# Token stages with centring and variance as 64x64 blocks in four tiles of the array, and token products padded to 128 rows

## The chip, the cores and the metric

The kernel runs on one core of one Trainium2 chip. The metric is the device time of one execution in microseconds (us). TensorE (PE in the profile) does the matrix products, its weight loads stand apart as PEld; ScalarE is ACT, VectorE is DVE, GpSimd is POOL, and SyncE (SP) issues nearly all DMAs.

## What is computed

The reference is a block of two layers over an image of 4 x 48 x 128 x 128. Each layer is a convolution part and a token part; the change touches the token part, which is the same for both layers:

```python
x = x + _L0_conv_ref(_ln_c(x), ...)
t = _to_tokens(x)                                  # B, H*W, C = 48 channels per token
t = t + _L0_ffn_ref(_ln_t(t), W1, b1, W2, b2)
x = _from_tokens(t, x)
x = x + _L1_conv_ref(_ln_c(x), ...)
...
def _ln_t(v, eps=1e-05):                           # over the 48 channels
    m = jnp.mean(v, axis=-1, keepdims=True)
    s = jnp.var(v, axis=-1, keepdims=True)
    return (v - m) / jnp.sqrt(s + eps)

def _qlinear(x, W, b):                             # 8-bit floats in, 16-bit floats out
    y = q_acc(jnp.einsum('bsk,nk->bsn', q_mul(x), q_mul(W)))
    return q_acc(y + q_mul(b))
h = jax.nn.relu(_qlinear(x, W1, b1))               # 48 -> 192
y = _qlinear(h, W2, b2)                            # 192 -> 48
```

## The kernel before

The program is a row of stages, each with its own buffers and a barrier of all engines behind it: `expand`, `gated_conv`, `token_mix` ("mix0"), `wavelet`, `attention_maps`, `fusion`, and `token_mix` again ("mix1"). Only `token_mix` changes. I call its two calls the first and the second token stage. The first is `wide` (its source has 96 rows) and has a second layer norm over its result, `"out"`, whose output feeds the wavelet stage; the second has the norm `"in"` only.

A token stage works through 2N = 64 tiles of 512 tokens. A tile holds two images at once: channels of one on partitions 0 to 47, of the other on 64 to 111 (`PADH` = 64, `CP` = 112). For one tile these pieces run, each on one engine:

- `project` (PE): the projection of the conv part into `x1_bank`; `add_residual` (DVE) adds the input and gives `x1`.
- `centre_in` (PE, L871): a 112x112 product with `center` subtracts the mean over each image's 48 channels; `square` (ACT, L934); `variance("in")` (PE, L889): a 112x112 product with `average`, into `x1_bank` again; `root` (ACT, L941 and L944): Ln and Exp give the reciprocal root; `quantize_norm` (DVE, L1030) multiplies and rounds to 8 bits, `xq`.
- `hide(0)`, `hide(1)` (PE, L902): 48 to 192 for both images, four products of 96 output rows, each into a bank of its own out of `bank` (two banks in the first stage, four in the second); `round_hidden` (ACT, L951) copies each bank to 16 bits; `bias_hidden` (DVE, L1036) and `quantize_hidden` (DVE, L1046) give `hq`.
- `show` (PE, L914): four accumulating products back to 48 channels in `x2_bank`; `round_shown` (ACT, L957); `add_shown` (DVE, L1052, L1057) adds `x1` and gives `x2`, which SP stores.
- in the first stage also `centre_out` (PE, L877), `square("out")`, `variance("out")` (PE, L889, into `x2_bank`), `root("out")` and `normalise` (DVE, L1066).

`staged` sets the order. Every engine walks over steps; in step k it takes its pieces in the order of the list `pieces`, each with the tile k minus that piece's stage number. So one step holds one piece of each kind, of different tiles, and each engine's order within a step is fixed by hand:

```python
pieces = [(0, project), (3, show), (2, hide(0)), (4, centre_out), (2, hide(1)), (1, variance("in")), (5, variance("out")), (0, centre_in)]
```

The engines wait for one another only by counting semaphores, written ahead of each piece (`pe.wait_ge(...)`). Which wait holds which piece decides the length of a step. Ahead of the loop DVE fills paddings with zeros, the last fill (L981) raises `prepared`, and SP, which waits for it, then issues the weights' DMAs and behind them the first tile's.

## Time and profile before

| | |
|---|---|
| median of 3 runs | 2580.16 us (2574.28 to 2590.53) |
| the profiled execution, its own time | 2568.33 us |
| its span, first to last instruction | 2566.5 us |
| mean granted TensorE clock, share of full speed | 0.94 |
| PE, DVE, ACT, POOL busy | 88%, 59%, 46%, 17% of the span |
| first token stage | about 793 to 1275 us |
| second token stage | about 2203 to 2566 us |

The profiled execution lies 2.18 us above its span. A busy share is a mean over stages with different limits, so it is read stage by stage: the timeline of one step of either token stage tells which engine waits there, and for what.

### The profile page before, as it was taken

How to read it: one execution, taken by the hardware profiler on the slowest of the kernel's cores; microseconds unless marked ns; L12 is line 12 of the kernel's file. 1: busy time of each engine (PE TensorE's matmuls, PEld its weight loads, DVE VectorE, ACT ScalarE, POOL GpSimd, SP SyncE). 2: the span in 40 equal slices, each digit the busy share in tenths (PEclk: the TensorE clock that was granted, in tenths of full speed). 3: DMA queues.
4: the chain of work that ended last, by engine and by line, in shares of the span. 5: the costliest groups of instructions: out<-in, count | busy, mean ns of one | idle time of the engine just before them, and what ended most of it. 6: DMA issues, size and time to landing. Idle time of an engine off the chain costs nothing. (4 is left out here: it accounts for less than half of the span.)

```text
span 2566.5 us, 61875 instructions
## 1 busy us (share of the span) xinstructions
PE 2261.6 (88%) x21290; PEld 1261.1 (49%) x21290; DVE 1521.9 (59%) x2653; ACT 1175.5 (46%) x2386; POOL 448.9 (17%) x707
## 2 busy tenths in 40 slices
PE   7679859999996999999699999999984999699997
PEld 3335517785783333333266666666651342233333
DVE  3335501111113777777578888888871555488887
ACT  4346422222222888888622222222220221388887
POOL 7610006101100000000044444444420000000000
PEclk9789859999997999999899999999996999799999
DMA  6999987787754778777486666666635999344343
GB/s 151 263 253 271 244 283 236 272 268 240 262 190 93 142 144 153 141 146 149 88 159 144 145 145 145 145 145 145 143 88 125 244 263 268 111 114 116 111 114 89
DMA packets 529401, 445.99 MB, mean 174 GB/s; under 512 B 315708, under 2 KB 444676, under 8 KB 525938
## 3 DMA queue, kind: packets, MB, share of 16 engines
q1 hardware_dynamic: 459042, 413.28, 62.6%
q0 software_dynamic: 5744, 23.34, 3.6%
q10 hardware_dynamic: 64512, 7.88, 2.3%
q8 instruction: 79, 1.29, 0.2%
q14 instruction: 24, 0.20, 0.0%
HBM read 259.75 MB, written 186.40 MB: 174 GB/s over the span
## 5 line engine op out<-in xcount | busy, mean ns | idle before, releaser
L602 PE MATMUL gate_ps<-gate_data,gate_wt 64*64 64x289 f32 x6144 | 389.2, 410 | 25.7 <-issue 18.9
L602 PEld LDWEIGHTS gate_ps<-gate_data,gate_wt 64*64 64x64 f32 x6144 | 306.3, 134 | 109.8 <-issue 39.4
L663 DVE TENSOR_TENSOR gate_out<-gate_gelu,gate_ps 128x578 f32<-128x578 f32 x96 | 72.2, 756 | 378.3 <-PE gate_ps L602 339.2
L951 ACT CAST mix_h<-mix_bank 96x512 f16<-96x512 f32 x512 | 267.5, 591 | 10.4 <-PE mix_bank L902 6.6
L640 ACT ACTIVATE gate_gelu<-gate_ps 128x578 f32<-128x578 f32 x96 | 62.8, 654 | 295.0 <-PE gate_ps L602 275.6
L1036 DVE TENSOR_SCALAR mix_hb<-mix_h,mix_b1q 96x1024 f16<-96x1024 f16 x256 | 122.8, 480 | 98.2 <-ACT mix_h L951 98.2
L2043 PE MATMUL fus_bank<-fus_xt,fus_taps 76*32 76x512 f32 x1344 | 156.0, 613 | 26.0 <-DMA fus_shift<-gate_shift 23.5
L902 PE MATMUL mix_bank<-mix_xq,mix_w1q 112*96 112x512 fp8e5 x512 | 143.5, 382 | 38.3 <-ACT mix_h L951 23.0
L1046 DVE CAST mix_hq<-mix_hb 96x2048 fp8e5<-96x2048 f16 x128 | 156.5, 1223 | 22.1 <-DVE mix_hb L1036 20.2
L292 DVE COPY exp_out<-exp_y 128x384 f32<-128x384 f32 x192 | 102.2, 567 | 104.8 <-PE exp_y L255 53.6
L255 PE MATMUL exp_y<-exp_win,exp_xb 48*128 48x192 f32 x1024 | 117.7, 369 | 48.8 <-DVE exp_out L292 30.0
L914 PE MATMUL mix_x_bank<-mix_hq,mix_w2q 96*112 96x512 fp8e5 x512 | 136.1, 388 | 5.5 <-DVE mix_hq L1046 3.5
L871 PE MATMUL mix_centre_in<-mix_x,mix_center 112*112 112x512 f32 x256 | 134.4, 607 | 2.1 <-DVE mix_x L1019 1.2
L255 PEld LDWEIGHTS exp_y<-exp_win,exp_xb 48*128 48x128 f32 x1024 | 92.5, 205 | 88.1 <-ACT exp_out L292 53.3
L1524 PE MATMUL wav_full_bank<-wav_halves,wav_base_w 80*32 80x256 f32 x2304 | 135.4, 381 | 0.0
L889 PE MATMUL mix_x_bank<-mix_sq_in,mix_average 112*112 112x512 f32 x256 | 132.8, 601 | 2.1 <-DVE mix_x L1019 1.2
L957 ACT CAST mix_y<-mix_x_bank 112x512 f16<-112x512 f32 x128 | 75.0, 586 | 105.6 <-PE mix_x_bank L914 105.6
L902 PEld LDWEIGHTS mix_bank<-mix_xq,mix_w1q 112*96 112x96 fp8e5 x512 | 52.6, 122 | 141.1 <-issue 118.0
L1465 PE MATMUL wav_front<-wav_strips,wav_front_w 48*32 48x256 f32 x3840 | 117.1, 383 | 0.0
L1670 POOL TENSOR_TENSOR wav_pool<-wav_scaled,wav_diag 128x256 f32<-128x256 f32 x96 | 68.8, 738 | 262.0 <-ACT wav_scaled L1579 261.8
L2043 PEld LDWEIGHTS fus_bank<-fus_xt,fus_taps 76*32 76x32 f32 x1344 | 50.5, 111 | 127.3 <-issue 127.1
L866 PE MATMUL mix_x_bank<-mix_sc,mix_proj 112*112 112x512 f32 x128 | 73.0, 652 | 45.1 <-ACT mix_logv_in L941 23.9
(227 smaller groups left out, 4103.5 us busy)
## 6 DMA issues: line engine op xcount, KB each, us to landing
y<-exp_out SPq DMA_DIRECT2D x64, 816.0 KB, 12.1
gate_data<-y SPq DMA_DIRECT2D x24, 2176.0 KB, 18.8
g<-gate_out SPq DMA_DIRECT2D x48, 578.0 KB, 4.5
mix_sc<-g SPq DMA_DIRECT2D x31, 816.0 KB
wav_strips<-xp SPq DMA_DIRECT2D x96, 204.0 KB, 3.9
wav_halves<-xp SPq DMA_DIRECT2D x48, 340.0 KB
init<-wav_init SPq DMA_DIRECT2D x48, 268.0 KB, 2.4
fus_xt<-init SPq DMA_DIRECT2D x24, 536.0 KB
```

Source lines behind the costliest of these rows:

```text
L255: mm = pe.matmul(ps_y[h][q % 2][:, O2 * x:O2 * (x + 1)], xb[u][rows, 2 * q + x].rearrange("c s y x -> c (s y x)"), win[rows, :], start=Tru ...
L602: mm = pe.matmul(banks(a, v)[64 * g:64 * (g + 1), r], wt[q][64 * r:64 * (r + 1), 2 * a + g, n, :], src, start=n == 0, stop=n == 3)
L871: pe.matmul(centre_bank["in"][at.pair][0:CP, :], center[:, :], x1[at.slot][:, :], start=True, stop=True).then_inc(centered["in"], 1)
L889: pe.matmul(var_bank[v][0:CP, :], average[:, :], sq[v][at.pair][:, :], start=True, stop=True).then_inc(var[v], 1)
L902: pe.matmul(bank[(2 * m + h) % len(bank)][0:HID, :], w1q[:, h, m, :], xq[at.pair][:, :], start=True, stop=True).then_inc(hidden, 1)
L914: mm = pe.matmul(x2_bank[0:CP, :], w2q[:, h, m, :], hq[at.pair][:, m, h, :], start=(h + m == 0), stop=(h + m == 2))
L951: act.copy(h16[at.pair][:, m, h, :], bank[(2 * m + h) % len(bank)][0:HID, :]).then_inc(h16_ready, 1)
L1036: relu = dve.tensor_scalar(hb[at.pair][:, m, :, :].rearrange("p h n -> p (h n)"), h16[at.pair][:, m, :, :].rearrange("p h n -> p (h n)"), ...
L1046: dve.tensor_copy(hq[at.pair][:, :, :, :].rearrange("p m h n -> p (m h n)"), hb[at.pair][:, :, :, :].rearrange("p m h n -> p (m h n)"), sa ...
L1465: x = pe.matmul(half(u, r, 0, Q0)[STRIP * g:STRIP * (g + 1)], front_w[u][64 * r:64 * r + K0, 2 + dx, :], strips[u][64 * r:64 * r + K0, g, ...
L1524: x = pe.matmul(images(full_bank[u][STRIP * g:STRIP * (g + 1), :])[:, :, e::2], base_w[u][:, e, dx, :], halves[u][:, g, :, 1 + dx:1 + dx + ...
L2043: mm = pe.matmul(bank[u][0][STRIP * s:STRIP * (s + 1), :], taps[u][0:K2, dx, :], xt[u][:, s, :, dx:dx + W], start=dx == 0, stop=dx == TAPS ...
```

## The change

Two facts stay as they are: the tiles, the stage numbers of the pieces and the order of ACT and DVE. What differs:

- `center` and `average` become 128x128, and each 112x112 product becomes two 64x64 blocks, one per image. `variance` uses the blocks that keep an image on its half of the partitions (rows 0 to 63 into partitions 0 to 63, rows 64 to 127 into 64 to 127). `exchange`, used for both centrings, uses the other two: rows 0 to 63 go into partitions 64 to 127 and the reverse, so the halves swap places. The weights of `hide` and the store of the second norm swap back.
- An instruction that only raises `pe_turn` stands ahead of each pair of blocks and takes the wait upon itself.
- On PE in the first stage `variance("out")` moves from behind `variance("in")` to directly behind `hide(0)`, ahead of `centre_out`.
- The banks of `hide` become pairs of adjacent banks. One pair holds both images of one m, ACT copies it in one instruction of 1024 columns where it had two of 512, and `hidden` and `h16_ready` are raised once for a pair.
- `xq` and `hq` get 128 partitions, and `w1q` and `w2q` 128 rows, the additional ones zero; `sq`, `x1`, `x2` get 128 partitions too.
- For that DVE has new fills ahead of the one that raises `prepared`: `center`, `average`, and 32 partitions of each buffer of `x1`, `x2`, `xq`, `hq`.

```diff
+                def exchange(v, at, x):
+                    pe.sem_inc(pe_turn, 1)
+                    pe.matmul(centre_bank[v][at.pair][PADH:128, :], center[0:PADH, 0:PADH], x[0:PADH, :], start=True, stop=True)
+                    pe.matmul(centre_bank[v][at.pair][0:PADH, :], center[PADH:128, PADH:128], x[PADH:128, :],
+                              start=True, stop=True).then_inc(centered[v], 1)
+
                 def centre_in(at):
                     pe.wait_ge(x1_ready, at.n + 1)
-                    pe.matmul(centre_bank["in"][at.pair][0:CP, :], center[:, :], x1[at.slot][:, :],
-                              start=True, stop=True).then_inc(centered["in"], 1)
+                    exchange("in", at, x1[at.slot])
...
                         pe.wait_ge(squared[v], at.n + 1)
-                        pe.matmul(var_bank[v][0:CP, :], average[:, :], sq[v][at.pair][:, :],
+                        pe.sem_inc(pe_turn, 1)
+                        pe.matmul(var_bank[v][0:PADH, :], average[0:PADH, 0:PADH], sq[v][at.pair][0:PADH, :], start=True, stop=True)
+                        pe.matmul(var_bank[v][PADH:128, :], average[PADH:128, PADH:128], sq[v][at.pair][PADH:128, :],
                                   start=True, stop=True).then_inc(var[v], 1)
...
-        bank = [k.ps(f"bank{j}") for j in range(8 - 2 - 2 * len(norms))]
+        pairs = [k.ps(f"bank{j}", (128, 2 * NT)) for j in range(3 - len(norms))]
...
-                        if m == 1 and len(bank) == 2:
-                            pe.wait_ge(h16_ready, 4 * at.n + 2)
+                        if m == 1 and len(pairs) == 1:
+                            pe.wait_ge(h16_ready, 2 * at.n + 1)
                         pe.sem_inc(pe_turn, 1)
                         for h in range(2):
-                            pe.matmul(bank[(2 * m + h) % len(bank)][0:HID, :], w1q[:, h, m, :], xq[at.pair][:, :],
-                                      start=True, stop=True).then_inc(hidden, 1)
+                            mm = pe.matmul(pairs[m % len(pairs)][0:HID, NT * h:NT * (h + 1)], w1q[:, 1 - h, m, :],
+                                           xq[at.pair][:, :], start=True, stop=True)
+                        mm.then_inc(hidden, 1)
...
-                        for h in range(2):
-                            act.wait_ge(hidden, 4 * at.n + 2 * m + h + 1)
-                            act.copy(h16[at.pair][:, m, h, :], bank[(2 * m + h) % len(bank)][0:HID, :]
-                                     ).then_inc(h16_ready, 1)
+                        act.wait_ge(hidden, 2 * at.n + m + 1)
+                        act.copy(h16[at.pair][:, m, :, :].rearrange("p h n -> p (h n)"), pairs[m % len(pairs)][0:HID, :]
+                                 ).then_inc(h16_ready, 1)
...
-                    pieces = [(0, project), (3, show), (2, hide(0)), (4, centre_out), (2, hide(1)), (1, variance("in")), (5, variance("out")), (0, centre_in)]
+                    pieces = [(0, project), (3, show), (2, hide(0)), (5, variance("out")), (4, centre_out), (2, hide(1)), (1, variance("in")), (0, centre_in)]
...
+                dve.memset(center[:, :], 0.0)
+                dve.memset(average[:, :], 0.0)
+                for x in x1 + x2 + xq:
+                    dve.memset(x[96:128, :], 0.0)
+                for x in hq:
+                    dve.memset(x[96:128].rearrange("p m h n -> p (m h n)"), 0.0)
```

On PE, in the loop of the first token stage, one step before, from `show` on (`mix_bank` are the banks of `hide`, `mix_x_bank` is `x1_bank` or `x2_bank`):

```order
L914 MATMUL mix_x_bank<-mix_hq,mix_w2q 112x512 x4
L902 MATMUL mix_bank<-mix_xq,mix_w1q 96x512 x2
L877 MATMUL mix_centre_out<-mix_x,mix_center 112x512
L902 MATMUL mix_bank<-mix_xq,mix_w1q 96x512 x2
L889 MATMUL mix_x_bank<-mix_sq_in,mix_average 112x512
L889 MATMUL mix_x_bank<-mix_sq_out,mix_average 112x512
L871 MATMUL mix_centre_in<-mix_x,mix_center 112x512
```

And the same step of the changed kernel (L921 is `show`, L908 `hide`, L894 and L895 `variance`, L871 and L872 `exchange`):

```order
L921 MATMUL mix_x_bank<-mix_hq,mix_w2q 112x512 x4
L908 MATMUL mix_bank<-mix_xq,mix_w1q 96x512 x2
L894 MATMUL mix_x_bank<-mix_sq_out,mix_average 64x512
L895 MATMUL mix_x_bank<-mix_sq_out,mix_average 64x512
L871 MATMUL mix_centre_out<-mix_x,mix_center 64x512
L872 MATMUL mix_centre_out<-mix_x,mix_center 64x512
L905 ISA
L908 MATMUL mix_bank<-mix_xq,mix_w1q 96x512 x2
L894 MATMUL mix_x_bank<-mix_sq_in,mix_average 64x512
L895 MATMUL mix_x_bank<-mix_sq_in,mix_average 64x512
L871 MATMUL mix_centre_in<-mix_x,mix_center 64x512
L872 MATMUL mix_centre_in<-mix_x,mix_center 64x512
```

The variance of the second norm went ahead of `centre_out` and `hide(1)`, so that a variance and a centring now stand side by side twice in a step, where one full product and two others stood apart.

On DVE, the fills at the start of the second token stage in the changed kernel, down to the one that raises `prepared` (L993); before there were none of `mix_center`, `mix_average`, `mix_x`, `mix_xq` and `mix_hq`:

```order
L975 MEMSET mix_center 128x128
L976 MEMSET mix_average 128x128
L978 MEMSET mix_x 32x512 x10
L978 MEMSET mix_xq 32x128 x2
L980 MEMSET mix_hq 32x512 x2
L981 MEMSET mix_w1q 128x96
L982 MEMSET mix_w2q 128x112
```

Sixteen fills came in ahead of the old ones there; in the first stage they are twelve (`mix_x` x6).

## Rows read from the trace of the kernel before

**Rows 1.** The copy of L957, once per step: first token stage, then the second.
```profile
L957 ACT CAST mix_y<-mix_x_bank x64: 586/586/586, 827.2 to 1262.2; 112x512 f16<-112x512 f32 x64
...
L957 ACT CAST mix_y<-mix_x_bank x64: 567/586/587, 2238.5 to 2561.4; 112x512 f16<-112x512 f32 x64
```

**Rows 2.** Timeline, first token stage: start us, us, engine, line; idle before <- releaser.
```profile
1004.85 1.07 PE L914 MATMUL mix_x_bank<-mix_hq,mix_w2q 96*112 96x512 fp8e5 x4
...
1005.96 0.59 ACT L957 CAST mix_y<-mix_x_bank 112x512 f16<-112x512 f32 x1 [0.66 <-PE mix_x_bank L914]
...
1006.44 1.07 ACT L951 CAST mix_h<-mix_bank 96x512 f16<-96x512 f32 x2
...
1007.65 0.60 PE L902 MATMUL mix_bank<-mix_xq,mix_w1q 112*96 112x512 fp8e5 x2 [0.44 <-ACT mix_h L951]
...
1008.09 1.02 PE L889 MATMUL mix_x_bank<-mix_sq_in,mix_average 112*112 112x512 f32 x2
...
1009.15 0.69 ACT L941 ACTIVATE mix_logv_in<-mix_x_bank,mix_eps 112x512 f32<-112x512 f32 x1
1009.18 0.48 DVE L1036 TENSOR_SCALAR mix_hb<-mix_h,mix_b1q 96x1024 f16<-96x1024 f16 x1 [0.86 <-ACT mix_h L951]
...
1009.81 1.02 PE L871 MATMUL mix_centre_in<-mix_x,mix_center 112*112 112x512 f32 x2
...
1009.81 1.22 DVE L1046 CAST mix_hq<-mix_hb 96x2048 fp8e5<-96x2048 f16 x1 [0.15 <-DVE mix_hb L1036]
...
1010.41 0.67 ACT L941 ACTIVATE mix_logv_out<-mix_x_bank,mix_eps 112x512 f32<-112x512 f32 x1
...
1010.76 0.98 PE L860 MATMUL mix_x_bank<-mix_sc,mix_proj 96*48 96x448 f32 x4
...
1011.78 1.07 PE L914 MATMUL mix_x_bank<-mix_hq,mix_w2q 96*112 96x512 fp8e5 x4
```

**Rows 3.** Timeline, second token stage, one step.
```profile
2355.35 0.71 ACT L941 ACTIVATE mix_logv_in<-mix_x_bank,mix_eps 112x512 f32<-112x512 f32 x1
2355.50 0.48 DVE L1036 TENSOR_SCALAR mix_hb<-mix_h,mix_b1q 96x1024 f16<-96x1024 f16 x1 [0.41 <-ACT mix_h L951]
...
2356.17 1.22 DVE L1046 CAST mix_hq<-mix_hb 96x2048 fp8e5<-96x2048 f16 x1 [0.18 <-DVE mix_hb L1036]
...
2357.31 0.68 DVE L1030 TENSOR_TENSOR mix_xq<-mix_centre_in,mix_rstd_in 112x512 fp8e5<-112x512 f32 x1
...
2358.12 0.59 ACT L957 CAST mix_y<-mix_x_bank 112x512 f16<-112x512 f32 x1 [0.92 <-PE mix_x_bank L914]
2358.13 1.03 PE L902 MATMUL mix_bank<-mix_xq,mix_w1q 112*96 112x512 fp8e5 x4
2358.60 2.04 ACT L951 CAST mix_h<-mix_bank 96x512 f16<-96x512 f32 x4
...
2360.68 0.48 DVE L1036 TENSOR_SCALAR mix_hb<-mix_h,mix_b1q 96x1024 f16<-96x1024 f16 x1 [0.47 <-ACT mix_h L951]
```

**Rows 4.** Timeline of PE in the gated convolution, 600 to 606 us.
```profile
599.73 6.53 PE L602 MATMUL gate_ps<-gate_data,gate_wt 64*64 64x289 f32 x104
```

**Rows 5.** Groups by form, ACT: out<-in shapes xcount | busy us, mean ns | idle.
```profile
L635 ACT COPY gate_wt<-gate_wt 64x1024 f32<-64x1024 f32 x48 | 50.1, 1044 | 1.2
```

**Rows 6.** Timeline, start of the second token stage (SPq is SP's queue of DMA issues).
```profile
2205.08 0.48 DVE L976 MEMSET mix_rs<- 32x512 f32 x1
2205.62 0.48 DVE L980 MEMSET mix_sc<- 32x512 f32 x1
2206.21 0.48 DVE L981 MEMSET mix_x_bank<- 32x512 f32 x1
2206.73 0.37 SPq L763 DMA_DIRECT2D mix_center<-in_consts_dram  x1
```

**Rows 7.** Windows: stretch, length, busy us (count) of PE, PEld, DVE, ACT, POOL; clock; DMA share, GB/s.
```profile
818.00:821.40 3.40, 2.00 (x13) 0.89 (x13) 2.06 (x4) 2.11 (x4) 0.00 (x0) 1.00 0.02 4
821.40:824.80 3.40, 3.40 (x6) 1.11 (x4) 1.86 (x3) 2.19 (x4) 0.00 (x0) 0.51 1.20 184
```

49 lines of the change are left out of this document (24 added, 25 removed).

## The prediction

> **What bounds the kernel now.** Only the two token stages change, so I read only these, and first how long a step of each is. L957 runs once per step: 64 times from 827.2 to 1262.2 us in the first stage, 435.0/63 = 6.90 us a step, and 322.9/63 = 5.13 in the second, fill and drain included [rows 1]. Then the timeline of one step, and in it who waits for whom.
>
> First stage, period 6.93 us (L914 at 1004.85 and at 1011.78) [rows 2]. PE is nearly full: `show` 1004.85, then without a gap `hide(0)` and `centre_out`, a wait of 0.44 at `hide(1)` for ACT's copies of `hide(0)`, then both variances and `centre_in` back to back, `project` at 1010.76, `show` again. A full 112x112 product holds the array for (1009.81 - 1008.09)/2 = 0.86. The chain that closes the step is: `show` to the copy L957, 1.11; that copy and the two of L951, 1.55, ending at 1007.51; `hide(1)` 0.14 later; 0.44 for its two products; three full products, 2.67 with the 0.09 explained below; `project` 1.02. Centring and variance are three of its links.
>
> Second stage, period 5.18 (L1036 at 2355.50 and 2360.68) [rows 3]. Here they are on no chain. From the last copy of `hide` the work goes through DVE: L1036, 0.67 later L1046, 1.14 later L1030, 0.82 later `hide` at 2358.13; and through ACT: L941 at 2355.35, `project`, `show`, L957 at 2358.12, four copies from 2358.60. Both arrive within half a microsecond of one another, and ACT's copies close the step: 2360.68 - 2358.60 = 2.08.
>
> **Blocks in four tiles.** The gated convolution of this kernel uses 64x64 products in four tiles: 104 records of 289 columns in 6.53 us, 0.063 each [rows 4]. A record of a full product (it has two, 0.43 each by 0.86/2 [rows 2]) scaled to 289 columns is 0.24, so there nearly four run at a time. If variance and centring do the same side by side, the four blocks take 0.86, and I add 0.03 for their staggered starts: 0.89 where two full products took 1.72. The bounds are 0.86 and 1.72. I take 0.89, since the nearest rows have this very tile size.
>
> Going from one tiling to another has a price. `centre_in` (full array) to `project` (column halves) is 1010.76 - 1009.81 = 0.95 where two full products are 0.86 apart [rows 2]: 0.09. In the first stage the switches rise from two to five in a step.
>
> **The first stage, new step.** I count from the start of `show`, with the rows' intervals [rows 2].
> - L957 starts at 1.11 and ends at 1.70. `variance("out")` writes the bank that it reads and so waits for it; PE answers an ended copy after 0.14 (1007.51 to 1007.65): 1.84. This wait is new: queued behind it are `centre_out` and all of `hide(1)`.
> - Four blocks 0.89 and a switch 0.09: `hide(1)` at 2.82. ACT's wide copy of `hide(0)` is over by then (next item): starts at 1.11 + 0.48 = 1.59, ends 2.63, answered at 2.77. The wait shown before at `hide(1)` is thus replaced by the new one.
> - `hide(1)` 0.60, and ACT 0.04 later: the second wide copy at 3.46. One copy of 1024 columns took 1.04 elsewhere [rows 5]; two of 512 took 1.07 with their overlap [rows 2]. I take 1.04 long and 0.93 (0.11 less, as 0.59 and 0.48 of a narrow one) until ACT starts the next. It ends at 4.50.
> - DVE: L1036 at 4.53, L1046 0.63 later at 5.16, over at 6.38, `show` 0.12 after that: **6.50**.
> - The other branches are shorter. `variance("in")` starts at 2.82 + 0.44 + 0.09 = 3.35 and is complete after 1.02 at 4.37; ACT starts L941 at 4.41, 1.26 later the second L941 at 5.67, over at 6.34. `project` follows the first L941: 4.41 + 0.69 + 0.05 = 5.15, and `show` could start at 6.17.
>
> So of 2 x 0.83 saved on PE, 0.43 of the step is left, and the bound moves from PE to a chain that runs over ACT and DVE. 63 x (6.93 - 6.50) = **-27 us**. Bounds: 6.35 if the answers of PE and DVE are quicker by 0.15 in all, 6.65 if the tile group and its switches cost 0.15 more: -37 to -18.
>
> **The second stage, new step.** The products saved here lie beside ACT's work and are worth nothing; PE only waits longer for L941. The pairs cost something: ACT's first copy needs both products of a pair. Chain over DVE [rows 3]: 0.67 + 1.14 + 0.82, then both products and ACT's answer, 0.64, then 0.93 for the first wide copy, 1.04 for the second and 0.03 for DVE: 5.27, against 5.18 now, where the first narrow copy starts 0.47 after `hide`. The chain over ACT: 2358.60 - 2355.35 = 3.25, and 2 x 0.93: 5.11. So 60 steps x 0.09 = **+5 us**; -4 if the chain over ACT were the only one, +10 if a wide copy were just two narrow ones (2 x 0.96 and 0.61 at the end).
>
> **The fills.** A fill of 32 x 512 takes 0.54 until the next [rows 6]. SP's first DMA stands 0.04 behind the last fill, so nothing hides them: the weights' DMAs, the first tile's and the first product all shift. In the first stage six of `x1` and `x2` and two of `hq`: 8 x 0.54; the narrow ones of `xq`, `center` and `average`, a quarter as long by my estimate, 4 x 0.14: 4.9. In the second stage twelve wide ones: 7.0. Together **+12 us** (10 to 14).
>
> The 128 rows of the token products cost nothing: before, 96 rows (L914) and 112 rows (L902) both have 1.03 for four products (in [rows 3] and, with the switch ahead of it, 1.07 in [rows 2]), so the row count doesn't show. ACT's squares over 128 partitions cost nothing either, since all partitions go through side by side; I bound that at 0.
>
> Sum: -27 + 5 + 12 = -10. On the profiled execution's own 2568.3 us that is 2558; on the median of 2580.2 it is **2570 us**. That median lies 12 above the profiled execution and its three runs are 16 apart, so about 1%, 26 us, is what a measurement can tell from no change.
>
> **Rivals.** *(a) Same, with a shorter chain.* DVE's tail from the wide copy to `show` is what I trust least, since it comes from intervals in which DVE was partly waiting. If ACT alone set the steps, the first stage would have 6.34 + 0.05 less the 0.09 of a quicker group, 6.30, and the second 5.11: -40 - 4 + 12 = -32, 2548 us. Against it: L1046 cannot start before both halves are rounded, and it takes 1.22 [rows 2].
>
> *(b) The tiles run two at a time: slower.* The rows of the gated convolution have different banks for the two row halves. Here the two blocks of a variance come from different row halves and write one bank, on different partitions; so do those of a centring. If such blocks had to follow one another, a group would take 1.72, `hide(1)` would start 0.83 later and the step be 7.33: 63 x 0.40 + 5 + 12 = +42, **2622 us**. The Trainium skill, "TensorEngine Tiling (Array Packing)", Restrictions and Gotchas, states that different row tiles cannot access the same PSUM bank at the same time, and that software must see to it. By that rule case (b) or an error would come; no row of this trace has two row tiles in one bank, so it is neither borne out nor refuted. The gain is gone from a group of 1.05 on (a step of 6.93 - 17/63 = 6.66), and from 1.46 on the kernel is slower by 1% (7.07).
>
> *(c) Half overlap.* The second pair starts only when the first pair's second record starts, held back by the instruction on `pe_turn` between them: a group of 1.32, a step of 6.93, no gain: 0 + 5 + 12 = +17, 2597 us.
>
> *(d) The clock.* With PE less busy, the granted clock may fall in the steady part. Where the first stage fills, PE was busy for 2.00 of 3.40 us, and behind that stretch the clock stood at 0.51, that is 1.2 GHz, for 3.4 us [rows 7]. In the second stage PE would now work 0.89 less of each 5.27 us. At 1.2 GHz `project` and `show`, which lie on the chain, take some 1.7 longer; if half of the steps met that, 30 x 1.7 = 51 on top: 2621 us. Against it: the gaps are at most 1.3 us long each, and the whole chain over ACT has slack of 0.16 first.
>
> **How the numbers follow.** Forecast 0.62 (own range 2549 to 2586 by the bounds: -37 - 4 + 10 to -18 + 10 + 14), (a) 0.13, (b) 0.10, (c) 0.09, (d) 0.06. Faster by over 1% means below 2554: all of (a) and a tenth of my own, 0.21. Slower means above 2606: (b) and (d), 0.16. Within 1%: 0.63. The range takes in my case, (c) and most of (a): 2545 to 2600.
>
> **What would show it.** Records of L894, L895, L871 and L872 that start within 0.1 us of each other, four at a time, with (b) and (c) wrong; step 6.5 in the first stage and 5.27 in the second, by the copy of 112x512; idle time of PE ahead of L894 put down to L963, and of `show` (L921) to DVE; `hide`'s copies as 256 of 1024 columns with some 1040 ns; the first product of each stage 5 and 7 us later after the barrier. I would be wrong if PE's wait ahead of L894 stayed near zero, if ACT had no idle time left in the first stage, or if the granted clock left 1.00 in either steady part.

## The result

| | before | after |
|---|---|---|
| median of the runs | 2580.5 us (2574.28 to 2590.53, 4 runs) | 2610.39 us (2598.77 to 2617.36, 4 runs) |
| the profiled execution, its own time | 2568.33 us | 2598.77 us |
| its span | 2566.5 us | 2597.0 us |
| mean granted clock | 0.94 | 0.935 |
| PE, DVE, ACT busy | 88%, 59%, 46% | 83%, 59%, 45% |

The ratio of the times is 1.0108, with a 95% interval of 1.0058 to 1.0158: slower by 1.1%, where 2570 us was forecast and 2600 was the upper end of the range. PE has 5% of the span less to do, and nothing came of it.

### The profile page after: what moved, and what is told of

It is laid out like the page before. It is cut to its first block and busy times, and to the rows that moved or that the text cites. A ratio compares the mean times of both kernels' runs of the same rounds, so it can differ in the third digit from the quotient of the medians.

```text
span 2597.0 us, 63153 instructions
## 1 busy us (share of the span) xinstructions
PE 2150.3 (83%) x22058; PEld 1189.7 (46%) x22058; DVE 1534.3 (59%) x2681; ACT 1168.9 (45%) x2130; POOL 448.2 (17%) x707
## 5 line engine op out<-in xcount | busy, mean ns | idle before, releaser
L602 PEld LDWEIGHTS gate_ps<-gate_data,gate_wt 64*64 64x64 f32 x6144 | 322.9, 134 | 96.4 <-issue 42.5
L957 ACT CAST mix_h<-mix_bank 96x1024 f16<-96x1024 f32 x256 | 252.0, 1009 | 15.3 <-PE mix_bank L908 11.4
L908 PE MATMUL mix_bank<-mix_xq,mix_w1q 128*96 128x512 fp8e5 x512 | 148.9, 394 | 10.1 <-DVE mix_xq L1042 4.8
L921 PE MATMUL mix_x_bank<-mix_hq,mix_w2q 128*112 128x512 fp8e5 x512 | 138.1, 393 | 21.3 <-ACT mix_logv_out L948 15.1
L871 PE MATMUL mix_centre_in<-mix_x,mix_center 64*64 64x512 f32 x256 | 143.0, 640 | 2.3 <-DVE mix_x L1031 1.3
L894 PE MATMUL mix_x_bank<-mix_sq_in,mix_average 64*64 64x512 f32 x256 | 141.2, 633 | 2.3 <-DVE mix_x L1031 1.3
L872 PE MATMUL mix_centre_in<-mix_x,mix_center 64*64 64x512 f32 x256 | 143.1, 640 | 0.0
L895 PE MATMUL mix_x_bank<-mix_sq_in,mix_average 64*64 64x512 f32 x256 | 141.3, 633 | 0.0
L860 PE MATMUL mix_x_bank<-mix_sc,mix_proj 96*48 96x448 f32 x256 | 65.6, 589 | 90.1 <-DMA mix_sc<-g 61.5
L963 ACT CAST mix_y<-mix_x_bank 112x512 f16<-112x512 f32 x128 | 74.9, 585 | 88.4 <-PE mix_x_bank L921 88.4
## 6 DMA issues: line engine op xcount, KB each, us to landing
y<-exp_out SPq DMA_DIRECT2D x64, 816.0 KB, 12.2
```

Source lines behind the costliest of these rows:

```text
L602: mm = pe.matmul(banks(a, v)[64 * g:64 * (g + 1), r], wt[q][64 * r:64 * (r + 1), 2 * a + g, n, :], src, start=n == 0, stop=n == 3)
L871: pe.matmul(centre_bank[v][at.pair][PADH:128, :], center[0:PADH, 0:PADH], x[0:PADH, :], start=True, stop=True)
L872: pe.matmul(centre_bank[v][at.pair][0:PADH, :], center[PADH:128, PADH:128], x[PADH:128, :], start=True, stop=True).then_inc(centered[v], 1)
L894: pe.matmul(var_bank[v][0:PADH, :], average[0:PADH, 0:PADH], sq[v][at.pair][0:PADH, :], start=True, stop=True)
L895: pe.matmul(var_bank[v][PADH:128, :], average[PADH:128, PADH:128], sq[v][at.pair][PADH:128, :], start=True, stop=True).then_inc(var[v], 1)
L908: mm = pe.matmul(pairs[m % len(pairs)][0:HID, NT * h:NT * (h + 1)], w1q[:, 1 - h, m, :], xq[at.pair][:, :], start=True, stop=True)
```

## The profile after

First how long the steps are. The copy of `show`'s result (L963 now), once per step, in the first and then the second token stage:

```profile
L963 ACT CAST mix_y<-mix_x_bank x64: 585/585/586, 837.1 to 1282.3; 112x512 f16<-112x512 f32 x64
L963 ACT CAST mix_y<-mix_x_bank x64: 567/585/594, 2266.6 to 2591.8; 112x512 f16<-112x512 f32 x64
```

Against [rows 1] the first stage takes 445.2 us from first to last copy where it took 435.0, and the second 325.2 where it took 322.9. Single steps tell more: in the first stage most last 6.83 or 7.0 to 7.6 us, with a mean of 7.04 without the first and last four, and 8.14 at most. Before, 43 of these 55 were 6.93 and the others up to 7.26.

The timeline of one such step, from `show` to `show`, for PE (the columns are as in [rows 2]):

```profile
1004.42 1.04 PE L921 MATMUL mix_x_bank<-mix_hq,mix_w2q 128*112 128x512 fp8e5 x4 [0.35 <-ACT mix_logv_out L948]
1005.30 0.59 PE L908 MATMUL mix_bank<-mix_xq,mix_w1q 128*96 128x512 fp8e5 x2
...
1006.23 0.61 PE L894 MATMUL mix_x_bank<-mix_sq_out,mix_average 64*64 64x512 f32 x1 [0.34 <-ACT mix_y L963]
...
1006.38 0.61 PE L871 MATMUL mix_centre_out<-mix_x,mix_center 64*64 64x512 f32 x1
...
1007.39 0.63 PE L908 MATMUL mix_bank<-mix_xq,mix_w1q 128*96 128x512 fp8e5 x2
...
1007.95 0.64 PE L894 MATMUL mix_x_bank<-mix_sq_in,mix_average 64*64 64x512 f32 x1
...
1007.96 0.64 PE L895 MATMUL mix_x_bank<-mix_sq_in,mix_average 64*64 64x512 f32 x1
...
1007.97 0.64 PE L871 MATMUL mix_centre_in<-mix_x,mix_center 64*64 64x512 f32 x1
...
1007.97 0.64 PE L872 MATMUL mix_centre_in<-mix_x,mix_center 64*64 64x512 f32 x1
...
1009.08 0.69 ACT L948 ACTIVATE mix_logv_in<-mix_x_bank,mix_eps 112x512 f32<-112x512 f32 x1
...
1010.33 0.67 ACT L948 ACTIVATE mix_logv_out<-mix_x_bank,mix_eps 112x512 f32<-112x512 f32 x1
1010.33 0.99 PE L860 MATMUL mix_x_bank<-mix_sc,mix_proj 96*48 96x448 f32 x4 [1.29 <-DMA mix_sc<-g]
...
1011.37 0.85 PE L921 MATMUL mix_x_bank<-mix_hq,mix_w2q 128*112 128x512 fp8e5 x3
```

Three things stand in it. The four blocks of the second group start within 0.02 us, so four tiles of the array do work side by side, two into each of two banks. In the first group `centre_out` starts 0.15 behind `variance("out")`, and `hide(1)` (1007.39) stands 2.97 behind `show`, where 2.82 was forecast. And `project` waits 1.29 us, in the end for SP's fetch of its source: ACT's Ln (L948, 1009.08) that it also waits for is over at 1009.77, so some 0.5 of the 1.29 is the fetch's alone. That wait is none of the prediction's. What ended PE's idle time ahead of L860 (us, times), after:

```profile
  ACT mix_logv_in L948: 127.2, 87
  DMA mix_sc<-g: 68.1, 30
```

24.5 of the 68.1 are the first tile. The other 29 are nearly every second step: the source of two tiles is fetched at once. SP's queue in the same stretch:

```profile
1000.53 0.86 SPq L818 DMA_DIRECT2D x<-mix_x  x2
1001.60 0.90 SPq L827 DMA_DIRECT2D xp<-mix_xn  x2
1003.15 0.34 SPq L788 DMA_DIRECT2D mix_sc<-g  x1
```

The fetch stands behind the stores of `x2` and of the norm, and those wait for DVE. So there is a loop over two steps: from `project` 3.8 to 4.4 us until the `x2` of that step ends, from there 2.4 to 2.8 until the fetch is issued, and from the issue 7.0 to 7.6 until the next but one `project`. Together that is 13.6 to 14.5 for two steps, 7.04 a step in the mean. Before, `x2` ended 3.8 to 4.0 behind `project`, and from the issue to the next but one `project` it was 7.2 to 7.6 us. In the step of [rows 2] that `project` starts at 1010.76, and its fetch was issued here:

```profile
1003.31 0.34 SPq L788 DMA_DIRECT2D mix_sc<-g  x1
```

That is 7.45. The loop was already on the edge there: of 23 fetches in the steady part, 12 landed 0.12 to 0.13 us ahead of the `project` that uses them, and that is also what separates landing and `project` after, where PE does wait (21 of 23). The fetch landed 7.22 us (median) behind its issue before and 7.26 after, so it has not become slower; two steps of 6.93 and the loop were equally long.

The second stage, rows that answer to [rows 3]:

```profile
2370.98 0.59 ACT L963 CAST mix_y<-mix_x_bank 112x512 f16<-112x512 f32 x1 [0.92 <-PE mix_x_bank L921]
...
2371.63 1.92 ACT L957 CAST mix_h<-mix_bank 96x1024 f16<-96x1024 f32 x2
...
2374.19 1.11 PE L866 MATMUL mix_x_bank<-mix_sc,mix_proj 112*112 112x512 f32 x2 [1.14 <-ACT mix_logv_in L948]
```

The first wide copy starts 0.65 behind the copy of `show` where the first narrow one stood 0.48 behind; a step is 5.22 for 5.17.

The start of the second stage, answering to [rows 6]: ten fills of `x1` and `x2` in one row, and SP's first DMA 10.66 us behind the stage's start (ACT's table load at 2222.9), where it was 3.42.

```profile
2223.52 5.35 DVE L978 MEMSET mix_x<- 32x512 f32 x10
2228.84 0.31 DVE L978 MEMSET mix_xq<- 32x128 uint32 x2
2229.20 1.03 DVE L980 MEMSET mix_hq<- 32x512 uint32 x2
...
2233.57 0.37 SPq L763 DMA_DIRECT2D mix_center<-in_consts_dram  x1
```

Last the clock. Windows from 16 us behind the start of the first token stage on, after (the columns are as in [rows 7]):

```profile
810.30:818.30 8.00, 2.97 (x12) 1.07 (x12) 1.13 (x2) 0.00 (x0) 0.00 (x0) 0.50 0.65 106
...
834.30:842.30 8.00, 6.61 (x22) 1.89 (x18) 3.90 (x8) 2.81 (x4) 0.00 (x0) 0.50 0.21 50
842.30:850.30 8.00, 6.23 (x36) 2.25 (x37) 5.78 (x10) 6.44 (x10) 0.00 (x0) 1.00 0.18 46
```

Before, the clock was at 1.00 at 818 us [rows 7] (it had risen 22 us behind the start of the stage, by shorter windows) and stayed there but for one dip of 3.4 us. After, it stands at 0.50, that is 1.2 GHz, for 48 us; and in the steady part it falls once more for 3.4 us, at 1180.2, behind the longest wait for a fetch (1.67 us). The step of 8.14 is that one.

The two profiled executions are 30.5 us apart. From the rows: first DMAs 5.1 and 7.2 later; from first DMA to first copy of `show` 3.6 and 1.3 longer (34.1 for 30.5, and 33.0 for 31.8); from first to last copy 10.2 and 2.3 longer; together 29.7, and 0.8 for all else.

## The experiments

All times below stand beside runs of the kernel before on the same chip; its medians were 2586.8 to 2589.1 us there. Two edits come back in many kernels. **Fills behind**: the fills of `x1`, `x2`, `xq` and `hq` stand behind the one that raises `prepared`.

```diff
-                for x in x1 + x2 + xq:
-                    dve.memset(x[96:128, :], 0.0)
-                for x in hq:
-                    dve.memset(x[96:128].rearrange("p m h n -> p (m h n)"), 0.0)
...
                 dve.memset(x1_bank[32:64, :], 0.0).then_inc(prepared, 1)
+                for x in x1 + x2 + xq:
+                    dve.memset(x[96:128, :], 0.0)
+                for x in hq:
+                    dve.memset(x[96:128].rearrange("p m h n -> p (m h n)"), 0.0)
                 dve.wait_ge(weights_in, 16 * (9 if wide else 12))
```

**Early fetch**: the source of the next two tiles is fetched with the loads of the odd tile, one step earlier. The wait on `x1_ready` that stands ahead of those loads already frees the buffer. One fetch too many, at the end, is waited for.

```diff
-                    if wide and at.pair == 0:
+                    if wide:
...
+                    if wide and at.pair == 1:
+                        share = (at.slot // 2 + 1) % 2
+                        fetch(share, 0, slice(0, SHARE) if share else slice(SHARE, 2 * SHARE),
+                              at.quad + 1).then_inc(src_in[share], 16)
...
+                        sp.wait_ge(src_in[u], 16 * (2 * N // 4 + 1 - u))
```

What the profiles gave, in us. "Step" is the median distance of the once-per-step copies without the first and last four; "first copy" counts from the stage's start (its table load), "1st to last" from that copy to the stage's last.

| kernel | ratio to before (95%) | first stage: first copy | step | 1st to last | second: first copy | step |
|---|---|---|---|---|---|---|
| before | 1 | 34.2 | 6.93 | 435.0 | 35.2 | 5.17 |
| after | 1.0108 (1.0058 to 1.0158) | 42.9 | 7.01 | 445.2 | 43.7 | 5.22 |
| fills_behind | 1.0065 (1.0031 to 1.0100) | 38.0 | 7.01 | 452.7 | 36.3 | 5.22 |
| early_fetch | 1.0024 (0.9979 to 1.0070) | 42.1 | 6.83 | 434.2 | 42.1 | 5.22 |
| before_early_fetch | 0.9958 (0.9925 to 0.9990) | 34.0 | 6.93 | 433.4 | 35.0 | 5.17 |
| blocks_alone | 1.0052 (1.0020 to 1.0085) | 41.6 | 7.06 | 443.6 | 41.6 | 5.17 |
| blocks_two_edits | 0.9944 (0.9912 to 0.9976) | 37.7 | 6.61 | 420.4 | 36.1 | 5.17 |
| after_both | 0.9990 (0.9959 to 1.0022) | 38.1 | 6.83 | 435.7 | 35.2 | 5.22 |
| order_back | 0.9936 (0.9903 to 0.9968) | 38.0 | 6.55 | 415.6 | 36.4 | 5.22 |
| narrow_back | 0.9981 (0.9947 to 1.0014) | 37.6 | 6.83 | 432.2 | 36.3 | 5.17 |
| unpad_back | 1.0069 (1.0037 to 1.0102) | 41.9 | 6.83 | 438.4 | 40.6 | 5.22 |
| waits_hoisted | 1.0021 (0.9992 to 1.0049) | 38.4 | 6.86 | 436.1 | 35.1 | 5.22 |
| turn_gone | 0.9976 (0.9931 to 1.0020) | 38.3 | 6.72 | 432.6 | 36.5 | 5.22 |
| after_warm | 1.0137 (1.0092 to 1.0183) | 42.1 | 7.01 | 454.4 | 43.3 | 5.22 |
| before_fetch_warm | 0.9977 (0.9946 to 1.0009) | 34.8 | 6.93 | 433.4 | 31.4 | 5.17 |
| best_warm | 0.9889 (0.9860 to 0.9919) | 37.0 | 6.55 | 411.7 | 35.8 | 5.17 |
| best_cold | 0.9878 (0.9811 to 0.9946) | 36.6 | 6.55 | 412.1 | 36.1 | 5.17 |
| full_var_start | 0.9877 (0.9814 to 0.9941) | 34.6 | 6.55 | 416.1 | 34.5 | 5.17 |

### The fills: fills_behind

> The changed kernel with one edit: the fills of x1, x2, xq and hq stand behind the fill that raises `prepared`, where DVE waits 5.5 us for the weights' DMAs in any case. Theory (the fills cost what they delay): SP's first DMA of the first token stage moves from 8.74 us behind the stage's start to about 4.2, that of the second by about 6.4 us; 11 us less, 2599 us; steps unchanged at 7.0 in the first stage. Rival (the 30 us are in the steps and in the fills only by the way, since a later first tile also meets other DMA traffic and another clock): less than 5 us come back, 2606 us or more.

The first DMAs stand at 3.94 and 3.70 us behind the stages' starts (8.74 and 10.66 after), the first copies 4.8 and 7.4 earlier: 12.2 us, which the theory said. The median is 2600.7 us, the ratio 1.0065 for 1.0108. The profiled execution took 2626.34, the longest of its ten, with steps up to 8.87 us in the first stage: waits for the fetch, which the next group takes away, and with them the clock fell to 1.2 GHz for 3.4 us five times.

### The fetch: early_fetch and before_early_fetch

> The changed kernel with one edit: SP issues the fetch of the next two tiles' source (mix_sc<-g) at the end of the loads of the odd tile before, one step earlier than now, ahead of the stores of x2 and of the norm. Theory (a second bound that the prediction missed: x2, the stores on SP, the fetch, project and x2 again form a loop of some 14.1 us for two steps): PE's waits for mix_sc<-g vanish, the step of the first stage falls from 7.02 to the length of the chain over ACT and DVE, 6.83 to 6.87 us; 10 us less, 2600 us. Rival (the scatter of the steps between 6.83 and 8.1 comes from ACT and DVE, and PE's waits for the fetch only stand where another wait would): step stays at 7.0, 2610 us within 3.

> The kernel before with the same edit on SP. Theory: its step of 6.93 is set by PE and the loop over the fetch (13.7 to 13.9 for two steps) is just hidden, so nothing changes: step 6.93, ratio 1.00 within 0.003. Rival (the loop over the fetch set the step before as well): step falls below 6.88 and the time by over 3 us. If the first tile's loads come later by the added DMA, that costs under 1 us.

What ended PE's idle time ahead of L860 with the early fetch:

```profile
  ACT mix_logv_in L948: 134.9, 114
...
  DMA mix_sc<-g: 25.1, 1
```

The 29 waits within the stage are gone, only the first tile's is left. The step falls to a median of 6.83 with 7.06 at most, the stage from 445.2 to 434.2 us, 11.0 less (8.1 in the 55 middle steps, 3.0 in the last four): the theory holds, the rival (steps stay at 7.0) falls. The median of the runs is 2592.7 us where 2600 was expected. There is more in it than the median step. Without the first and last four, the longest steps in the five profiles of a kernel with the late fetch are 7.26 (before), 8.14, 8.87, 9.55 and 9.62; in the thirteen others, which have it early, none is above 7.27. Two things go together there. A step that waits for a DMA takes on the scatter of its landing, and in the four kernels with blocks and the late fetch the clock fell to 1.2 GHz for 3.4 or 6.8 us, one to six times, in the steady part; every step above 8.2 us holds such a fall. In the kernels with the early fetch it fell in none. The runs do not tell how much of the 11.0 is the wait and how much the clock behind it.

In the kernel before nothing was to change. The median step did not (6.93), the mean fell from 6.955 to 6.928, 1.6 us over the stage: the 12 steps above 6.95 are gone, so the loop did hold some steps there. The time fell by more than expected, and by more than these 1.6 us: 2577.8 beside 2587.4, a ratio of 0.9958, whose interval ends at 2.6 us. The expectation had put that (over 3 us) with the rival, whose other half, a step below 6.88, did not come. Where the rest comes from is open.

### Only the blocks: blocks_alone and blocks_two_edits

Here the pieces of PE have the order of before, the banks are single, the copies narrow, and the token products have 112 and 96 rows. The second kernel has fills behind and early fetch on top.

```diff
-pieces = [(0, project), (3, show), (2, hide(0)), (5, variance("out")), (4, centre_out), (2, hide(1)), (1, variance("in")), (0, centre_in)]
+pieces = [(0, project), (3, show), (2, hide(0)), (4, centre_out), (2, hide(1)), (1, variance("in")), (5, variance("out")), (0, centre_in)]
...
-                            mm = pe.matmul(pairs[m % len(pairs)][0:HID, NT * h:NT * (h + 1)], w1q[:, 1 - h, m, :],
-                                           xq[at.pair][:, :], start=True, stop=True)
+                            pe.matmul(bank[(2 * m + h) % len(bank)][0:HID, :], w1q[0:CP, 1 - h, m, :], xq[at.pair][0:CP, :],
+                                      start=True, stop=True).then_inc(hidden, 1)
```

> Of the change only the 64x64 blocks (with the swapped halves) are left: PE's order in a step is that of before, hide has single banks with narrow copies, the two token products have 112 and 96 rows, and the fills are those of center, average, x1 and x2. Theory (the loop over the fetch bounds what blocks can give): PE's work in a step falls by 0.86, the chain over DVE would close after 6.3 to 6.4, but two steps still last the 13.9 to 14.1 of the loop over the fetch, so 6.95 to 7.05 a step in the first stage, second stage 5.15 to 5.2; with 10 us of fills 2588 to 2600 us. Rival (the wide copies and the new order cost the time, and the blocks alone give what the prediction wanted): step 6.4 to 6.6, 2560 to 2572 us.

> The kernel with the blocks alone (order, banks, copies and row counts of before) and both edits that took away a delay: the early fetch of mix_sc and the fills behind `prepared`. Theory (the blocks shorten the chain, and only the loop over the fetch hid that): the step of the first stage falls from 7.03 in the mean to that kernel's shortest, 6.57 us, so the stage's last copy stands 63 x 0.36 = 22 us nearer to its first than before (435 us there, 413 here), the second stage stays at 5.17, the first DMA of each stage at 3.9 us; 2560 us beside 2587 of the kernel before on this chip. Rival (the blocks alone also need the new order and the wide copies to gain, as they were written together): step 6.8 or more, 2578 us or more.

Alone, the blocks gain nothing: 7.03 in the mean, with steps as short as 6.57 and as long as 9.55, and 2606 us (2588 to 2600 was expected). `x2` ended 3.8 to 4.0 behind `project` here, as in the kernel before, and the loop over the fetch is 14.06 all the same. With the fetch out of the way the same blocks give 6.61, 420.4 us from first to last copy for 435.0, 2565.8 beside 2586.8 us. The expected 413 and 2560 were a little too good, since I had taken the shortest step for the mean. This is the plainest pair of the study: the sign of the result turns. The second kernel also has its fills behind, which is 9.0 us at the first DMAs; but fills lie ahead of the steps and leave them as they are (7.01 in fills_behind), so the 23.2 us from first to last copy belong to the fetch.

### Which part of the rest costs: after_both, order_back, narrow_back, unpad_back

The first is the changed kernel with both edits. The next two undo one part on top of that: the order of PE's pieces (the first hunk above), or the pairs with their wide copies. unpad_back undoes the 128 rows and has the early fetch only, so it is read against early_fetch.

> The changed kernel with the early fetch and the fills behind `prepared`, and nothing else. Theory: both delays are gone and the step is the chain's 6.83 to 6.89, the first DMAs of the stages stand at 3.9; 2587 to 2592 us, within 0.3% of the kernel before on this chip: the blocks as the change orders them gain nothing even then, since 63 x 0.08 is given back by the slower start. Rival: 2575 us or less, if the two delays together hid more than apart.

> The changed kernel with early fetch and fills behind `prepared`, and the variance of the second norm back at its old place behind the first variance. Theory (the new order puts a wait for the copy of show, the variance, the centring and 0.15 us for the second wait between hide(0) and hide(1): hide(1) starts 2.97 behind show): hide(1) then waits only for the wide copy of hide(0), 2.75 to 2.8 behind show, and the step falls from 6.83 to 6.60 to 6.70. Rival (the order gains, since four tiles side by side take half the time of two groups of two): step above 6.9.

> The changed kernel with early fetch and fills behind `prepared`, and single banks with copies of 512 columns in place of the pairs with copies of 1024. Theory (the wide copy starts only behind both products, but saves ACT 0.1): ACT's first copy of hide(1) starts 0.3 earlier, two copies take 1.07 against 1.01, so the step of the first stage falls from 6.83 to 6.55 to 6.65 and that of the second from 5.22 to 5.17. Rival (ACT is short of time, the wide copy gains): step 6.9 or more in the first stage.

> The changed kernel with the early fetch alone, and the two token products with 112 and 96 rows again and without the fills of xq and hq. Theory (the row count of a product shows nowhere): step 6.83 to 6.89 in the first stage and 5.22 in the second, as with the early fetch alone; first DMA of the first stage 1.4 us earlier, 7.4 behind the stage's start; 2591 us. Rival (the zeros on 16 and 32 more rows cost clock, as the array switches more): the stretch at 1.2 GHz at the start of the first stage, 48 us with 128 rows, falls to 30 us or less, and 3 us or more come back.

after_both: 0.9990, 2590.0 us, as expected. With both delays away the change as written is where the kernel before is. **The order** is what costs: put back, the step falls from 6.83 to 6.55, 20 us over the stage, more than expected. From `show` to `show` in order_back:

```profile
1000.98 1.04 PE L921 MATMUL mix_x_bank<-mix_hq,mix_w2q 128*112 128x512 fp8e5 x4 [0.34 <-ACT mix_logv_out L948]
...
1002.39 0.64 PE L871 MATMUL mix_centre_out<-mix_x,mix_center 64*64 64x512 f32 x1
...
1003.70 0.60 PE L908 MATMUL mix_bank<-mix_xq,mix_w1q 128*96 128x512 fp8e5 x2 [0.24 <-ACT mix_h L957]
...
1005.36 0.69 ACT L948 ACTIVATE mix_logv_in<-mix_x_bank,mix_eps 112x512 f32<-112x512 f32 x1
...
1006.61 0.67 ACT L948 ACTIVATE mix_logv_out<-mix_x_bank,mix_eps 112x512 f32<-112x512 f32 x1
...
1007.54 0.61 PE L921 MATMUL mix_x_bank<-mix_hq,mix_w2q 128*112 128x512 fp8e5 x2 [0.35 <-ACT mix_logv_out L948]
```

`centre_out` no longer waits for the copy of `show`; it runs while PE would wait for ACT's wide copy anyway, and `hide(1)` stands 2.72 behind `show` for 2.97. The variance of the second norm now takes a turn of its own behind the first (0.9 us in which only two tiles work) and that costs nothing, since ACT can use its result only 1.25 later. A group of four tiles is the shorter way for PE and the longer way for the step.

**The wide copies** are neither good nor bad in the first stage (6.83 with and without) and cost 0.05 a step in the second. The expectation for the first stage was wrong: I had the step closed by DVE behind the second copy, but it is closed by `variance("in")`, the two Ln and `show`, on which the copies do not lie. **The 128 rows** cost nothing but their fills: 6.83 and 5.22 in both, and the clock stood at 0.50 as long. The ratio of unpad_back, 1.0069, is above early_fetch's 1.0024 with intervals that meet; its median, 2602.0 us, is above the 2591 that was expected, while its profile is only 0.2 us longer.

### Why 6.83 and not 6.50: waits_hoisted and turn_gone

Both start from after_both. The first moves the waits, the second also drops one instruction.

```diff
                 def centre_out(at):
-                    pe.wait_ge(x2_ready, at.n + 1 + SLOTS)
-                    pe.wait_ge(xn_ready, at.n + 1)
+                    if isinstance(at.n, int):
+                        pe.wait_ge(x2_ready, at.n + 1 + SLOTS)
+                        pe.wait_ge(xn_ready, at.n + 1)
...
+                            pe.wait_ge(x2_ready, capped(at.n + 2, 2 * N) + SLOTS)
+                            pe.wait_ge(xn_ready, capped(at.n + 2, 2 * N))
                             pe.wait_ge(y16_ready, capped(at.n + 3, 2 * N) + 1)
...
-                    pe.sem_inc(pe_turn, 1)
+                    if v == "in" or isinstance(at.n, int):
+                        pe.sem_inc(pe_turn, 1)
```

> The changed kernel with early fetch and fills behind `prepared`, and with PE's waits in another place: those of centre_out stand ahead of variance(out), so that nothing waits between the two groups, and the wait of show for hq stands last. Theory (the two terms of the chain that were sized too small: the second group starts 0.15 late, show answers after 0.25): step of the first stage falls from 6.83 to 6.55 to 6.70. Rival (0.15 and 0.25 are what PE takes from one tiling to the other and for the weights, whatever the waits): step stays within 0.03 of 6.83.

> As the kernel with the waits moved, and without the instruction that only raises pe_turn between variance(out) and centre_out. Theory (behind a wait PE's queue handles each such instruction in 0.10 to 0.11 us, whatever it waits for): the first record of the second group starts 0.05 instead of 0.15 behind the first group's, hide(1) 0.10 earlier, step 6.75 to 6.80. Rival (the 0.15 are the array's, which loads the blocks' weights one after another): second group still 0.12 or more behind, step 6.86.

Moving the waits did nothing: 6.86. My theory of the waits fell. The group of `variance("out")` in waits_hoisted, then in turn_gone:

```profile
1003.17 0.61 PE L897 MATMUL mix_x_bank<-mix_sq_out,mix_average 64*64 64x512 f32 x1 [0.54 <-ACT mix_y L966]
1003.18 0.64 PE L898 MATMUL mix_x_bank<-mix_sq_out,mix_average 64*64 64x512 f32 x1
1003.33 0.61 PE L871 MATMUL mix_centre_out<-mix_x,mix_center 64*64 64x512 f32 x1
...
1004.33 0.63 PE L911 MATMUL mix_bank<-mix_xq,mix_w1q 128*96 128x512 fp8e5 x2
```
```profile
1019.95 0.61 PE L898 MATMUL mix_x_bank<-mix_sq_out,mix_average 64*64 64x512 f32 x1 [0.40 <-issue]
1019.96 0.64 PE L899 MATMUL mix_x_bank<-mix_sq_out,mix_average 64*64 64x512 f32 x1
1019.96 0.64 PE L872 MATMUL mix_centre_out<-mix_x,mix_center 64*64 64x512 f32 x1
...
1020.97 0.63 PE L912 MATMUL mix_bank<-mix_xq,mix_w1q 128*96 128x512 fp8e5 x2
```

With the waits gone from between the groups, `centre_out` is 0.16 behind as before. With the instruction on `pe_turn` gone it is 0.01 behind, `hide(1)` comes 1.02 behind the group's first record for 1.16, and the step is 6.72 for 6.86. So the 0.15 belongs to that one instruction, which is more than the 0.10 that was expected of it. In the second group, where PE has no idle time in front, the same instruction costs nothing (L871 0.02 behind L894 after). My reading is that right behind a wait nothing is queued up yet, and PE's matrix work comes only as fast as its queue hands it over; no run shows that. What is left of 6.72 against 6.50 is mainly `show`: it starts 0.22 behind the end of the second Ln in turn_gone and waits_hoisted, 0.25 after, where 0.05 was forecast; two waits and the instruction on `pe_turn` stand ahead of it on PE, and I tried only their order.

### The slow start: after_warm, before_fetch_warm, full_var_start

In the first two, PE runs 36 products of zeros ahead of each token stage, which nobody reads.

```diff
+                pe.wait_ge(warmed, 1)
+                for _ in range(36):
+                    pe.matmul(x2_bank[:, :], warm[:, 0:128], warm[:, :], start=True, stop=True)
                 pe.wait_ge(quantized, 1)
```

> The changed kernel with one addition: in each token stage PE runs 36 products of zeros (8 bits, 128 rows, 512 columns, into x2_bank, read by nobody) while it waits for the weights and the first tile; at 0.43 us each at 1.2 GHz they last at most 15.5 us, and PE waits 19.7 in any case. Theory (the stages fill slower than before because the granted clock stays at 0.5 to 48 us behind the stage's start, where before it rose after 22): with PE busy from 1 us on the clock is at 1.0 when the first tile comes; the first copy of show comes at +38 in place of +42.9 in the first stage and at +39 in place of +43.7 in the second, about 10 us less in all, 2600 us. Rival (the first tiles of a stage are slow for their DMAs and waits, the low clock is a sign of it and no cause): the clock is high and the first copy comes no more than 1 us earlier; or the clock falls again in the first gaps.

> The kernel before with the early fetch and the same 36 products of zeros ahead of each token stage: what the fill of a stage is worth at the high clock without the blocks. PE waits 14.8 us there, so the last of the products may end 1 us behind the first tile's landing if the clock never rises. Theory: the first copy of show comes 2 to 4 us earlier in each stage (34.2 and 35.2 before), 2571 us beside 2587 of the kernel before. Rival: no change against the early fetch alone (2578).

The rival's second half came true. Windows of best_warm, which has the same products, from the start of its first token stage:

```profile
806.70:814.70 8.00, 7.71 (x30) 3.21 (x31) 6.74 (x23) 1.25 (x1) 0.00 (x0) 0.80 0.13 26
814.70:822.70 8.00, 2.01 (x10) 0.82 (x10) 1.83 (x10) 0.00 (x0) 0.00 (x0) 0.84 0.95 159
822.70:830.70 8.00, 5.43 (x20) 1.46 (x16) 2.26 (x4) 0.60 (x1) 0.00 (x0) 0.50 0.86 130
```

The clock is up after 4 us of products and down again before the first tile is worked on, and it then stays down as if nothing had been done. In after_warm the first copies come 0.8 and 0.4 us earlier, and nothing in the total. In before_fetch_warm the first stage's came 0.8 later; the second stage's came 3.7 us earlier, and there alone the clock stayed up, at 1.00 from 6.3 us behind the stage's start to its last steps. PE stood idle for 1.7 us there between the products of zeros and the first tile, and for 3.4 to 9.8 us in the other five stages that had such products. So a fast clock at the start is worth something where it lasts. The ratio, 0.9977 (2583 us where 2571 was expected), is still no better than without the products (0.9958).

> The best kernel without the products of zeros, and with the variances of the tiles that are written out (the first 12 steps of the first token stage, the first 8 of the second, and the last) as full 112x112 products. Theory (with four-tile groups the clock stays at 1.2 GHz to +45, where with full products it rose at +22, since the array does less at a time): the clock rises before +35, and the first copy of show comes 1 us or more earlier than +38.0. Rival (the clock answers to the waits between the first tiles, not to the kind of product): the clock rises where it did, and the first copy comes no earlier or later by up to 1 us, since the full products take longer.

In this kernel (order of before, wide copies in the first and narrow ones in the second stage, both edits) the tiles whose steps are written out have full products for their variances:

```diff
+                        if isinstance(at.n, int):
+                            pe.matmul(var_bank[v][0:CP, :], average[0:CP, 0:CP], sq[v][at.pair][0:CP, :],
+                                      start=True, stop=True).then_inc(var[v], 1)
+                            return
                         pe.matmul(var_bank[v][0:PADH, :], average[0:PADH, 0:PADH], sq[v][at.pair][0:PADH, :], start=True, stop=True)
```

Windows from 16 us behind the start of the first token stage, in best_cold (the same kernel with blocks throughout), then in full_var_start:

```profile
804.10:812.10 8.00, 5.36 (x24) 1.75 (x24) 2.26 (x4) 0.60 (x1) 0.00 (x0) 0.50 0.82 129
812.10:820.10 8.00, 6.13 (x24) 1.69 (x25) 2.31 (x4) 3.02 (x5) 0.00 (x0) 0.50 0.87 154
```
```profile
809.20:817.20 8.00, 5.36 (x20) 1.43 (x16) 2.26 (x4) 0.60 (x1) 0.00 (x0) 0.65 0.83 128
817.20:825.20 8.00, 6.52 (x23) 1.91 (x22) 3.49 (x6) 4.54 (x7) 0.00 (x0) 0.79 0.91 156
```

In the first 8 us PE is busy for the same 5.36 in both, and only in the second does the clock rise in them, as it did before. The first copies come at 34.6 and 34.5, 2.0 and 1.6 us earlier than in best_cold and as early as in the kernel before, although the products themselves are longer. The time of the rise scatters: order_back and best_cold have the same first stage, and the clock rose 47.6 and 33.8 us behind its start. But in the three kernels with full products and no products of zeros it first rose at 21.6 to 26.9 us (and fell back for 3.4 us at 28.4 in two of them), in eleven of the twelve with blocks at 33.8 to 55.6, and in the twelfth, early_fetch, at 26.7 for 3.4 us and then at 47.2. So the theory holds, as far as one profile of each kernel can tell: the blocks hold the clock low at the start. It is not yet a gain in the total (2558.0 beside 2560.4 us): the steps that are written out are longer with full products, up to 6.98, those at the stage's end too, and from first to last copy it takes 416.1 for 412.1.

### The best kernel: best_warm and best_cold

> What the runs before point to in one kernel: the blocks and wide copies in the first token stage with PE's order of before, narrow copies in the second, early fetch, fills behind `prepared`, and the products of zeros ahead of each token stage. Theory: step 6.55 in the first stage and 5.17 in the second, first copy of show at +33 to +34 in both in place of +38.0 and +36.4; 2569 less 3 for the second stage's steps and 6 for the faster start, 2560 us beside 2587 of the kernel before. Rival (the products of zeros change nothing of the start): 2566 us.

> The best kernel without the products of zeros. Theory: steps as there, 6.55 and 5.17; the start of the first token stage 1.0 us slower (first copy of show at +38.0 where it was +37.0) and of the second 0.6; 2560 us, within 0.2% of it. Rival (the products of zeros gave the 0.5% between order_back and best_warm): 2569 us.

Blocks, wide copies in the first stage and narrow ones in the second, PE's order of before, early fetch, fills behind: 2560.4 us, and with the products of zeros 2557.7, beside 2587 to 2589 of the kernel before. The ratios, 0.9878 and 0.9889, say that the products of zeros add nothing. Both beat the kernel before by 1.1 to 1.2%, and the changed one by about 2%. Part of that needs no blocks: with the early fetch alone the kernel before stands at 0.9958, and against that the blocks and wide copies are worth 0.8%. Step and second stage came out as expected (6.55, 5.17), the start did not: 37.0 and 35.8 where 33 to 34 was expected.

## Why the prediction was wrong, point by point

**The step that failed is "the first stage, new step": 6.50 us, and with it the term of -27 us.** The profile gave 7.04 and +10.2 us from first to last copy.
- What was missing is a bound outside the chain that I counted: the loop over SP and the fetch of `mix_sc`. It makes a mean step of 7.04 where the same kernel without it has 6.89, and gives back 11.0 us (early_fetch). I looked at who waits in one step of before, and PE showed no wait for that DMA in it; but the loop was as long as two steps there, and half of the fetches landed just in time. A shorter chain could gain nothing from then on. The new order is not needed for it: with the order of before the step is 7.03 (blocks_alone).
- The chain itself is 6.83. It closes through ACT's two Ln, a branch that was forecast at 6.39 beside 6.50 for DVE's; DVE ends 0.04 earlier now. Along that branch: the tile group with its switch 1.16 for 0.98, of which 0.14 is the instruction on `pe_turn` directly behind a wait (turn_gone); `show` 0.25 behind the Ln for 0.05; from `variance("in")` to the first Ln 1.13 for 1.06; the other terms within 0.03. Together 0.44, where the outer bound that I gave for the answers and for the group was 0.15.
- That ACT and DVE would bound the step and PE have idle time was right. That `variance("out")` ahead of `hide(1)` puts a new wait into the chain was right too, but I took the order as given and did not price it: it costs 0.28 a step (order_back against after_both), 20 us over the stage in the profiles.

**The second stage** was right in sign and too high in size: 5.22 for 5.17, +2.3 us from first to last copy where +5 was forecast, all from the wide copies (narrow_back). ACT needs 1.92 us for two wide copies and starts the second 0.91 behind the first, where 0.93 was taken.

**The fills** were right: 12.3 us at the first DMAs, 12.2 given back by fills_behind, +12 forecast.

**The 128 rows** cost nothing, as forecast (unpad_back).

**Rivals.** (b) and (c) are wrong: four blocks start within 0.02 us of one another. The Trainium skill, "TensorEngine Tiling (Array Packing)", Restrictions and Gotchas, says that different row tiles cannot access one PSUM bank at the same time. The trace disagrees for this case: L894 and L895, from different row halves into one bank on different partitions, start 0.01 apart, and the second records of both have ended 1.08 us later. (a), a shorter chain, is wrong. (d) had the right agent, mostly in the wrong place: in the steady part the clock left 1.00 once, for 3.4 us in the first stage and behind a wait for the fetch, and in the second not at all. At the start of the stages it stays at 1.2 GHz for 26 and 12 us longer. First DMA to first copy is 3.6 and 1.3 us longer with that; full_var_start, where the clock rises early again, took 2.0 and 1.6 us off such a start. No term of the sum stood for that. One sum of the chances is off: all of (a) and a tenth of my own are 0.19, not 0.21.

The sum again, with what was measured, for +30.5 between the profiled executions: chain 63 x (6.83 - 6.93) = -6.3; loop over the fetch +11.0; ends of the first stage and its longer fourth steps +5.5 (what is left of +10.2 there); second stage +2.3; fills +12.3; slow starts +4.9; all else +0.8.

**Left open.** With the new order every fourth step lasts 7.0 even with the early fetch; the loop body holds four tiles, so its own branch and address arithmetic is a candidate, not tried. Why the kernel before gains more from the early fetch than its profile shows is open too. Why a product of zeros brings the clock up in 4 us and four-tile groups do not in 40 is shown only as a fact. The last four steps of the first stage took 30.2 us after. The profiles tell two parts of that: with the new order they took 27.2 in the three kernels where the clock stayed at 1.00 to the last copy, and 28.0 to 30.2 in the six where it fell before; with the old order 26.0 to 26.2 (26.7 in full_var_start). So 1.2 is the order, and up to 3.0 goes with the clock. Why it falls there is not shown.

## What to carry to other kernels

Before counting what a shorter chain gives, look for loops that nobody waits for yet: for each transfer in the step, add issue, landing and the work until it can be issued again, and compare the sum with the steps that it has. If the data land just ahead of their use, every time by the same 0.12 us, that isn't slack, it is the next bound. And when an engine stops being the bound, an order that packs it well is worth nothing by itself: the pieces that others wait for come first, and no instruction that the queue must still hand over should stand between a wait and the work behind it.
